# Differential attention and gated layer: a new order of work in the slots, three shared or split PSUM banks, and the gated layer's first steps taken into the last slots

## The chip, the cores and the metric

One Trainium2 chip (trn2), one of its cores. The metric is the device time of one execution of the whole program in microseconds (us); lower is better. The five engines of a core are named as in the profile: PE (matmul; PEld is its weight load), DVE (vector), ACT (scalar), POOL (GpSimd) and SP, which here only issues DMAs.

## What is computed

The program runs six layers, one after the other, on x of 4096 rows of 256 numbers (128 sequences of 32 tokens): `x = x + layer(layernorm(x))`. The change touches two of them, the second (differential attention) and the third (a gated feed-forward with 4-bit weights):

```
def _L0_attn_ref(x, wq, wk, wv, wout, ...):          # 128 sequences of 32 tokens
    q = (x @ wq.T).reshape(b, t, NH2, HALF)           # 4 half heads of 64
    k = (x @ wk.T).reshape(b, t, NH2, HALF)
    v = (x @ wv.T).reshape(b, t, H, 2 * HALF)         # 2 heads of 128
    q = _apply_rope(q, cos, sin)
    k = _apply_rope(k, cos, sin)
    probs = jax.nn.softmax(einsum('bhtd,bhsd->bhts', q, k) / SCALING, axis=-1)
    diff = probs[:, :, 0] - lam * probs[:, :, 1]
    attn = jnp.einsum('bhts,bhsd->bhtd', diff, v)
    attn = attn * jax.lax.rsqrt(jnp.mean(attn * attn, axis=-1, keepdims=True) + EPS)
    return (attn * subln_weight) @ wout.T
...
def _L0_ffn_ref(x, weight1, weight2, weight3):        # the gated layer, 256 -> 704 -> 256
    w1, w2, w3 = (nf4_roundtrip(w) for w in (weight1, weight2, weight3))
    h = jax.nn.silu(x @ w1.T) * (x @ w2.T)
    return h @ w3.T
```

## The kernel before, in words

The rows of x are cut into 32 chunks of 128 rows, four sequences each (`CHUNKS`). Everything is float32; the rounded 4-bit weights come as bf16. Each layer is a `Phase` with one function for each engine, and these are called layer after layer, so every engine has one straight queue, written out by hand in program order; semaphores tie the queues together.

**Differential attention** (tiles ending in `_d`) is a software pipeline over slots n = -3 to 34 (`SLOTS`). In slot n the engines work on chunks n-2 to n+3 at once. PE does, in this order: `qk` (queries and keys of chunk n+1, L1613), `qk_t` (turns of the roped queries and keys of chunk n, L1621), `v` (L1626), `at` (turns of the weighed values of chunk n-2, L1634), `x` (turns of the normalized x of chunk n+2, L1640), `s` (scores of chunk n, L1650), `av` (weighing: the transposed probabilities of chunk n-1 times v, L1660) and `y` (output projection of chunk n-2, L1669). ACT copies PSUM to SBUF and does the exponentials and squares; DVE does rope, softmax, the layernorm's statistics (L1719 to L1721), the normalizing (L1726) and the residual sum (L1781); POOL does half of the rope (L1596, L1597) and two powers of -0.5, `inv_std` (L1600) for the layernorm and `inv_rms` (L1603) for the norm after the weighing. ACT's `attn` (L1677) scales the weighed values by `inv_rms`; `attn_t` (L1696) copies their turns for the output projection.

In the weighing each sequence s of 32 tokens and each head c is one 32x128 product. A product works on the 32 array rows of its sequence, and its place in the output (partitions 32s and up) picks the 32 array columns. Both heads of a sequence use the same 32x32 tile of the array: four tiles, each used twice.

**The gated layer** (tiles ending in `_g`) first turns its weights: 18 parts of W1, W2 and W3, each with PE transposes into a bank (L1917, L1920) and an ACT copy out (L2002 to L2006), four banks in turn. Then come the statistics of four chunks (`statistics`), POOL's powers, the normalizing, the turn of x (L1928, eight transposes), ACT's rounding copy (L2012) and DVE's remainder (L2092). Then the projections run for 8 turns of 512 rows: 11 tiles up (L1964, four matmuls each) and 6 parts down (L1985). PE begins all this only when the last `y_d` has been added (`pe.wait_ge(*before.high)`). SP loads the gated layer's x and weights in `preload`, called in slot 30 of the layer before.

## Time and profile before

| | us |
|---|---|
| median of 3 runs | 3342.03 (3341.38 to 3342.73) |
| the profiled execution | 3341.55 |
| its span, first to last instruction | 3339.5 |
| differential attention, first `qk` to last `y` | 906.2 to 1092.3 |
| gated layer's first up projection | 1099.5 |

All views below are of the profiled execution. Times are from the start of its span. "Granted clock" is the share of TensorE's full clock (2.4 GHz; the lower level is 1.2 GHz, shown as 0.50) that the chip gave it in a stretch. A timeline row is one group of like instructions in a row: start, length from the first start to the last end, engine, line, operation, output and inputs, and how many. Matmuls overlap their neighbours, so PE is read by the starts of its groups. A float32 matmul shows up as two records, which is why counts there are twice those of the program order. In square brackets stands how long the engine was idle before, and on whom it waited.

### The profile page before, as it was taken

Reading aid. Unit: us, or ns where it says so; the run is one execution under the profiler, and the core shown is the slowest. Engines: PE = TensorE matmul, PEld = TensorE weight load, DVE = VectorE, ACT = ScalarE, POOL = GpSimd, SP = SyncE. Lnnn points to the kernel's source line nnn. Section 1 sums busy time; section 2 is a strip of 40 time slices with the busy share of each in tenths; the row PEclk is TensorE's granted clock in tenths of the full one; section 3 lists DMA queues with packets and bytes.
Section 4 is the critical chain, followed back from the end, with each engine's and each line's share of the span. In section 5 each row is a group of like instructions: output and inputs, shape, how many; then the busy total and the mean of one; then the engine's idle time right before and its main releaser. Section 6 shows DMA issues by size and latency. Waiting matters only on the chain.

```text
span 3339.5 us, 103483 instructions
## 1 busy us (share of the span) xinstructions
PE 3287.2 (98%) x34647; PEld 2394.9 (72%) x34656; DVE 2329.3 (70%) x7527; ACT 1988.0 (60%) x6064; POOL 1796.8 (54%) x3701
## 2 busy tenths in 40 slices
PE   9999999999899999999999999999999999999999
PEld 7888888888666777777777777777766655555555
DVE  5677777777788667888888888878868844444443
ACT  5777777777556547777777777777765411111111
POOL 5666666666566447777777777777746500000000
PEclk9999999999999999999999999999999999999999
DMA  3111111111212231111111111111136720000000
GB/s 99 55 58 56 54 54 54 58 55 54 72 43 61 85 125 46 46 49 47 45 46 46 48 46 46 47 44 47 48 90 159 186 66 19 19 17 17 17 16 9
DMA packets 280202, 187.70 MB, mean 56 GB/s; under 512 B 117037, under 2 KB 276997, under 8 KB 280085
## 3 DMA queue, kind: packets, MB, share of 16 engines
q1 hardware_dynamic: 279797, 185.75, 19.9%
q8 instruction: 73, 1.20, 0.2%
q10 hardware_dynamic: 288, 0.40, 0.1%
q14 instruction: 44, 0.36, 0.0%
HBM read 145.61 MB, written 36.21 MB: 54 GB/s over the span
## 4 chain that ended last, share of the span: by engine, by line
PE 57%; DMA 3%; DVE 1%; ACT 0%; SPq 0%; issue 0%; POOL 0%; DVEq 0%; ACTq 0%; POOLq 0%
PE bank_e L2827 13%; PE c_ps_a L1100 7%; PE bank_e L2807 7%; PE b_ps_a L1066 6%; PE s_ps_a L1073 5%; PE out_ps_a L1126 3%; PE a_ps_a L1077 3%; PE c_ps_a L1077 2%; PE b_ps_a L1077 2%; PE out_ps_a L1110 2%; PE c_ps_a L1159 2%; DMA by_dim_q_r<-scratch_q 1%; PE c_ps_a L1138 1%; PE out_ps_a L1197 1%; PE c_ps_a L1149 1%; DMA scratch_q<-proj_t_q_r 1%
## 5 line engine op out<-in xcount | busy, mean ns | idle before, releaser
L1226 ACT ACTIVATE probs_a<-s_ps_a,neg_max_a 128x257 f32<-128x257 f32 x1024 | 473.7, 475 | 83.3 <-DVE neg_max_a L1346 78.5
L1280 POOL TENSOR_SCALAR probs_a<-probs_a,gated_a 128x256 f32<-128x256 f32 x1024 | 470.9, 479 | 26.4 <-POOL gated_a L1289 26.4
L1346 DVE TENSOR_REDUCE neg_max_a<-s_ps_a 128x1 f32<-128x257 f32 x1024 | 424.4, 414 | 0.0
L2870 ACT ACTIVATE gate_e<-bank_e 128x512 f32<-128x512 f32 x128 | 76.3, 597 | 486.1 <-PE bank_e L2827 459.1
L546 POOL TENSOR_SCALAR probs_i<-probs_i,inv_sum_i 128x256 f32<-128x256 f32 x512 | 242.9, 487 | 135.1 <-DVE inv_sum_i L710 130.6
L2768 POOL TENSOR_TENSOR inv_std_e<-var_eps_e,half_e 128x4 f32<-128x4 f32 x8 | 8.1, 1012 | 561.7 <-DVE var_eps_e L2884 561.7
L2994 DVE TENSOR_TENSOR hidden_e<-gate_e,bank_e 128x512 f32<-128x512 f32 x128 | 87.2, 687 | 277.5 <-PE bank_e L2827 274.8
L1345 DVE TENSOR_TENSOR self_s_a<-s_ps_a,mask_a 128x32 f32<-128x32 f32 x1024 | 186.1, 182 | 135.5 <-PE s_ps_a L1073 135.4
L530 ACT ACTIVATE probs_i<-s_ps_i,neg_max_i 128x257 f32<-128x257 f32 x512 | 235.8, 474 | 58.9 <-DVE neg_max_i L781 57.1
L373 PE MATMUL a_ps_i<-w_k_i,ctx_t_i 128*128 128x256 f32 x1024 | 252.4, 389 | 0.0
L1100 PE MATMUL c_ps_a<-w_v_a,ctx_t_a 128*32 128x256 f32 x4096 | 247.6, 382 | 0.0
L360 PE MATMUL c_ps_i<-w_v_i,ctx_t_i 128*128 128x256 f32 x1024 | 247.5, 379 | 0.0
L2827 PE MATMUL bank_e<-xn_t_e,w_gate_e 128*128 128x512 f32 x512 | 241.4, 594 | 0.0
L2827 PE MATMUL bank_e<-xn_t_e,w_up_e 128*128 128x512 f32 x512 | 240.6, 592 | 0.0
L1066 PE MATMUL b_ps_a<-ctx_t_a,w_qk_a 128*128 128x256 f32 x1016 | 240.5, 380 | 0.0
L2807 PE MATMUL bank_e<-w_down_e,hidden_e 128*128 128x256 f32 x1024 | 231.3, 379 | 0.0
L2807 PEld LDWEIGHTS bank_e<-w_down_e,hidden_e 128*128 128x128 f32 x1024 | 194.0, 190 | 50.0 <-issue 26.5
L781 DVE TENSOR_REDUCE neg_max_i<-s_ps_i 128x1 f32<-128x257 f32 x512 | 181.5, 416 | 50.9 <-PE s_ps_i L439 50.1
L1226 ACT ACTIVATION_READ_ACCUMULATOR probs_a<-s_ps_a,neg_max_a 128x1 f32 x1024 | 209.4, 205 | 0.0
L373 PEld LDWEIGHTS a_ps_i<-w_k_i,ctx_t_i 128*128 128x128 f32 x1024 | 184.4, 190 | 28.9 <-issue 0.4
L1100 PEld LDWEIGHTS c_ps_a<-w_v_a,ctx_t_a 128*32 128x32 f32 x4096 | 120.0, 109 | 115.2 <-issue 25.7
L1073 PE MATMUL s_ps_a<-k_t_a,q_bd_a 32*128 32x289 f32 x2048 | 197.6, 455 | 5.1 <-ACT probs_a L1226 3.1
(398 smaller groups left out, 8164.6 us busy)
## 6 DMA issues: line engine op xcount, KB each, us to landing
ctx_t_i<-in_ctx_t SPq DMA_DIRECT2D x128, 256.0 KB, 2.7
ctx_t_a<-in_ctx_t SPq DMA_DIRECT2D x128, 256.0 KB, 2.7
mask_a<-in_L_xattn_mask SPq DMA_DIRECT2D x512, 4.0 KB, 1.5
v_bd_a<-v_self_a SPq DMA_DIRECT2D x512, 8.0 KB, 1.8
x_tok_i<-in_x SPq DMA_DIRECT2D x32, 128.0 KB, 2.0
x_res_i<-in_x SPq DMA_DIRECT2D x32, 128.0 KB, 2.4
x_after<-y_tok_i SPq DMA_DIRECT2D x32, 128.0 KB, 1.8
x_tok_d<-x_after SPq DMA_DIRECT2D x32, 128.0 KB, 2.2
```

Source lines behind the costliest of these rows:

```text
L360: last = pe.matmul(c_ps[:, r * D:r * D + D], ctx_t[at.b(1)][:, c, r * P:r * P + P], w_v[:, c, :], start=c == 0, stop=c == 1)
L373: last = pe.matmul(a_ps[:, r * D:r * D + D], ctx_t[at.b(2)][:, c, r * P:r * P + P], w_k[:, c, :], start=c == 0, stop=c == 1)
L530: act.activation(probs[:, i, :], s_ps[i][:, 0:K], ACT.Exp, bias=neg_max[:, i:i + 1], accum_out=row_sum[:, i:i + 1]).then_inc(exp_done, 1)
L546: pool.tensor_scalar(probs[:, i, 0:2 * P], probs[:, i, 0:2 * P], inv_sum[:, i:i + 1], 1.0, ALU.mult, ALU.mult).then_inc(probs_ready, 1)
L1066: last = pe.matmul(into[:, f * n:f * n + n], w_qk[:, c, D + f * P:D + f * P + P], ctx[:, c, 0:n], start=c == 0, stop=c == 1)
L1073: pe.matmul(s_ps[:, g, 0:N], q_bd[j][rows, f, :, :].rearrange("p h q -> p (h q)"), k_t[j][rows, f, :], start=True, stop=True).then_inc(sco ...
L1100: last = pe.matmul(c_ps[32 * g:32 * g + 32, r * D:r * D + D], ctx_t[at.b()][:, c, r * P + 32 * g:r * P + 32 * g + 32], w_v[:, c, :], start ...
L1226: act.activation(probs[:, t, :], s_ps[:, g, 0:K], ACT.Exp, bias=neg_max[:, t:t + 1], accum_out=row_sum[:, t:t + 1]).then_inc(exp_done, 1)
L1280: pool.tensor_scalar(probs[:, t, 0:2 * P], probs[:, t, 0:2 * P], gated[:, t:t + 1], 1.0, ALU.mult, ALU.mult).then_inc(probs_ready, 1)
L1346: dve.tensor_reduce(neg_max[:, 4 * f + g:4 * f + g + 1], s_ps[:, g, 0:K], AX.X, ALU.max, negate=True).then_inc(max_ready, 1)
L2807: last = pe.matmul(w[:, t * D:t * D + D], hidden[e % 2][:, k, tok:tok + P], w_down[:, e, k, :], start=k == 0, stop=k == TILES - 1)
L2827: last = pe.matmul(w[:, :], weights[:, e, c, t * P:t * P + P], xn_t[:, c, :], start=c == 0, stop=c == 1)
```

## The change

It has four parts.

1. **Banks.** `av_ps` takes two banks, one for each head. `v_ps` and `y_ps` become the two halves of one bank, `vy_ps`. For that, PE's `v` waits until DVE has added the previous `y`, and PE's `y` waits until ACT has copied `v`; and DVE adds `y` right after `ms` and no longer at the end of its slot.
2. **Weighing.** Head 1 of sequence s goes to output partitions 32 x ((s+2) mod 4), so the eight products use eight different tiles. All eight now increase the semaphore (before, four did). The rows of head 1 stand rotated by two sequences in `attn`, which `attn_t` puts right: its one copy of 256 columns becomes two copies of 128. PE does `av` ahead of `s`.
3. **Start of the gated layer.** Its statistics and normalizing of four chunks stand in slots 29 to 32 of DVE and POOL, where the differential layer has none left. Six groups of weight turns (W1 and W2, two parts a group) and their ACT copies stand in slots 30 to 33, and the turn of the first x, ACT's rounding copy and DVE's remainder in slot 33. The W3 turns follow the last `y`; their ACT copies stand between the first SiLUs. The wait for the last `y_d` moves to the third up tile.
4. **SP.** `preload` of the gated layer moves from slot 30 to slot 27, and the second loads of x to slot 33.

```diff
-    qk_ps, v_ps, tx_ps, av_ps = (pb(f"{n}_ps") for n in ("qk", "v", "tx", "av"))
-    s_ps = pb("s_ps", (P, 2, 512))
-    qk_t_ps, y_ps = (pb(f"{n}_ps") for n in ("qk_t", "y"))
+    qk_ps, qk_t_ps, vy_ps, tx_ps = (pb(f"{n}_ps") for n in ("qk", "qk_t", "vy", "tx"))
+    av_ps, s_ps = (pb(n, (P, 2, 512)) for n in ("av_ps", "s_ps"))
+    v_ps, y_ps = vy_ps[:, 0:D], vy_ps[:, D:2 * D]
...
-            if n == CHUNKS - 2:
+            if n == CHUNKS - 5:
                 for j in range(2):
                     sp.wait_ge(stored[j], 16 * 4)
                 ahead.preload(sp)
+            if n == CHUNKS + 1:
+                ahead.second(sp)
...
+            elif n + 3 - CHUNKS in range(LANES):
+                ahead.pool(pool, n + 3 - CHUNKS)
...
+            if n == CHUNKS - 1:
+                ahead.weights[0](pe, 1)
+            if n == CHUNKS:
+                pe.wait_ge(qk_t_ready, CHUNKS)
+                ahead.weights[0](pe, 2)
+                ahead.weights[0](pe, 3)
+            if n == CHUNKS + 1:
+                ahead.weights[0](pe, 4)
+                ahead.weights[0](pe, 5)
+                pe.wait_ge(centred_ready, CHUNKS)
+                ahead.rows[0](pe, 0)
             if live(n + 1):
                 ge(pe, v_ready, n + 1)
+                ge(pe, y_ready, n - 2)
...
+                for s in range(4):
+                    own = slice(L * s, L * s + L)
+                    for c in range(2):
+                        across = (s + 2 * c) % 4
+                        last = pe.matmul(av_ps[L * across:L * across + L, c, 0:P], diff_t[(n - 1) % 2][own, c * L:c * L + L], v[(n - 1) % 3][own, c * P:c * P + P], start=True, stop=True)
+                        last.then_inc(av_full, 1)
...
                 pe.wait_ge(at_ready, n - 1)
                 ge(pe, y_ready, n - 2)
+                if live(n + 1):
+                    pe.wait_ge(v_ready, n + 2)
...
+            if CHUNKS - 1 <= n <= CHUNKS:
+                ahead.weights[1](act, 2 * (n - CHUNKS + 1))
+            if n == CHUNKS + 1:
+                ahead.weights[1](act, 4)
+                ahead.weights[1](act, 5)
...
+            if n == CHUNKS:
+                ahead.weights[1](act, 3)
+            if n == CHUNKS + 1:
+                ahead.rows[1](act, 0)
...
-                act.activation(attn_t[:, :, :].rearrange("p c k -> p (c k)"), at_ps, ACT.Copy).then_inc(at_ready, 1)
+                act.activation(attn_t_of[:, 0::3, :], at_of[:, 0::2, :], ACT.Copy)
+                act.activation(attn_t_of[:, 1:3, :], at_of[:, 1::2, :], ACT.Copy).then_inc(at_ready, 1)
...
+            if n == CHUNKS + 1:
+                ahead.rows[2](dve)
+            if live(n - 2):
+                dve.wait_ge(y_full, n - 1)
+                ge(dve, stored[n % 2], 16 * ((n - 2) // 2))
+                dve.tensor_tensor(y[n % 2][:, :], y_ps, x_tok[(n - 2) % X_TILES][:, :], ALU.add).then_inc(y_ready, 1)
...
+    W_BANKS = [bank[0], bank[0], bank[1], bank[0], bank[1], bank[0], down_ps[0], down_ps[0], down_ps[1]]
+    W_BEFORE = [None, 0, None, 1, 2, 3, None, None, None]
...
-        pe.wait_ge(*before.high)
-        pe.wait_ge(const_ready, 2)
-        for n in range(W_TURNS):
...
+        for group in range(6, 9):
+            turn_weights(pe, group)
...
+                if i == 0 and tile == 2:
+                    pe.wait_ge(*before.high)
...
                 silu(i, n)
+                if i == 0 and n < 3:
+                    copy_weights(act, 6 + n)
```

PE's order in a full slot, before and in the change. PE is the engine that is almost never idle there; `vy_ps_d` with `w_v` is `v`, with `w_o` is `y`.

```order
L1613 MATMUL qk_ps_d<-w_qk_d,xn_t_d 128x512 x2
L1621 MATMUL qk_t_ps_d<-ident_d,qk_d 128x128 x4
L1626 MATMUL v_ps_d<-w_v_d,xn_t_d 128x256 x2
L1634 MATMUL tx_ps_d<-ident_d,attn_d 128x128 x2
L1640 MATMUL tx_ps_d<-ident_d,xn_d 128x128 x2
L1650 MATMUL s_ps_d<-qk_t_d 32x32 x16
L1660 MATMUL av_ps_d<-v_d,diff_t_d 32x128 x8
L1669 MATMUL y_ps_d<-w_o_d,attn_t_d 128x256 x2
```

The same slot in the change:

```order
L1621 MATMUL qk_ps_d<-w_qk_d,xn_t_d 128x512 x2
L1629 MATMUL qk_t_ps_d<-ident_d,qk_d 128x128 x4
L1646 MATMUL vy_ps_d<-w_v_d,xn_t_d 128x256 x2
L1654 MATMUL tx_ps_d<-ident_d,attn_d 128x128 x2
L1662 MATMUL tx_ps_d<-ident_d,xn_d 128x128 x2
L1672 MATMUL av_ps_d<-v_d,diff_t_d 32x128 x8
L1682 MATMUL s_ps_d<-qk_t_d 32x32 x16
L1693 MATMUL vy_ps_d<-w_o_d,attn_t_d 128x256 x2
```

Only `av` and `s` have changed places.

PE at the end of the differential layer, from slot 32's `at` on, before:

```order
L1634 MATMUL tx_ps_d<-ident_d,attn_d 128x128 x2
L1660 MATMUL av_ps_d<-v_d,diff_t_d 32x128 x8
L1669 MATMUL y_ps_d<-w_o_d,attn_t_d 128x256 x2
L1634 MATMUL tx_ps_d<-ident_d,attn_d 128x128 x2
L1669 MATMUL y_ps_d<-w_o_d,attn_t_d 128x256 x2
L1917 MATMUL bank_g<-ident_bf_g,rows_g 128x128 x10
```

And in the change, down to the first up projection:

```order
L1654 MATMUL tx_ps_d<-ident_d,attn_d 128x128 x2
L1672 MATMUL av_ps_d<-v_d,diff_t_d 32x128 x8
L1693 MATMUL vy_ps_d<-w_o_d,attn_t_d 128x256 x2
L1973 MATMUL bank_g<-ident_bf_g,rows_g 128x128 x6
L1973 MATMUL bank_g<-ident_bf_g,rows_g 128x64 x2
L1983 MATMUL bank_g<-ident_g,xn_g 128x128 x4
L1654 MATMUL tx_ps_d<-ident_d,attn_d 128x128 x2
L1983 MATMUL bank_g<-ident_g,xn_g 128x128 x4
L1693 MATMUL vy_ps_d<-w_o_d,attn_t_d 128x256 x2
L1976 MATMUL bank_g<-ident_bf_g,cols_g 128x128 x10
L1976 MATMUL bank_g<-ident_bf_g,cols_g 64x128 x4
L2028 MATMUL bank_g<-xs_g,up_w_g 128x512 x44
```

The last W2 turns and both halves of the x turn have moved ahead of the last `y`; before, all of them, W1's too, followed it.

DVE in a slot of the drain (chunk 31's softmax), in the change:

```order
L1793 TENSOR_REDUCE top_d<-s_ps_d 128x4
L1794 TENSOR_TENSOR centred_d<-s_ps_d,top_d 128x128
L2132 BN_STATS stats_g<-x_tok_g 128x6
L2134 BN_AGGR mean_var_g<-stats_g 128x2
L2136 TENSOR_SCALAR var_eps_g<-mean_var_g 128x1
L1807 TENSOR_SCALAR ms_d<-ss_d 128x2
L1813 TENSOR_TENSOR y_d<-vy_ps_d,x_tok_d 128x256
L1819 TENSOR_REDUCE row_sum_d<-probs_d 128x4
```

Before, `ms_d` followed `centred_d` directly here, `row_sum_d` followed `ms_d`, and `y_d` came last.

## Rows read from the trace of the kernel before

**Rows 1.** Busy time by stretch: us, then each engine's busy time, clock, DMA.

```profile
920.00:1065.00 145.00, 144.47 (x1829) 98.88 (x1828) 118.77 (x397) 89.59 (x321) 100.51 (x107) 0.99 0.15 46
```

**Rows 2.** Timeline of a full slot, PE's groups: start, length, what.

```profile
1000.21 1.88 PE L1613 MATMUL qk_ps_d<-w_qk_d,xn_t_d 128*128 128x512 f32 x4
...
1003.45 0.38 PE L1640 MATMUL tx_ps_d<-ident_d,xn_d 128*128 128x128 f32 x2
...
1003.76 0.35 PE L1650 MATMUL s_ps_d<-qk_t_d 64*32 64x32 f32 x32
...
1004.04 0.65 PE L1660 MATMUL av_ps_d<-v_d,diff_t_d 32*32 32x128 f32 x16
...
1004.62 1.13 PE L1669 MATMUL y_ps_d<-w_o_d,attn_t_d 128*128 128x256 f32 x4
...
1005.59 1.45 PE L1613 MATMUL qk_ps_d<-w_qk_d,xn_t_d 128*128 128x512 f32 x3
```

**Rows 3.** The weighing's matmuls: ns min/median/max of one record.

```profile
L1660 PE MATMUL av_ps_d<-v_d,diff_t_d x512: 267/268/292, 923.3 to 1087.5; 32*32 32x128 f32 x171
```

**Rows 4.** The same slot's timeline: ACT, POOL and DVE.

```profile
1000.35 0.97 POOL L1600 TENSOR_TENSOR inv_std_d<-var_eps_d,half_d 128x1 f32<-128x1 f32 x1 [0.31 <-DVE var_eps_d L1721]
...
1001.30 0.70 POOL L1603 TENSOR_TENSOR inv_rms_d<-ms_d,half_d 128x2 f32<-128x2 f32 x1
...
1002.03 0.62 ACT L1677 ACTIVATE attn_d<-av_ps_d,inv_rms_d 128x128 f32<-128x128 f32 x2 [1.64 <-POOL inv_rms_d L1603]
...
1002.25 0.37 DVE L1726 TENSOR_SCALAR xn_d<-x_tok_d,mean_var_d,inv_std_d 128x256 f32<-128x256 f32 x1
...
1002.53 0.42 DVE L1781 TENSOR_TENSOR y_d<-y_ps_d,x_tok_d 128x256 f32<-128x256 f32 x1
1002.54 0.60 ACT L1682 ACTIVATE qk_raw_d<-qk_ps_d 128x512 f32<-128x512 f32 x1
...
1003.02 0.61 ACT L1685 ACTIVATE qk_t_d<-qk_t_ps_d 128x512 f32<-128x512 f32 x1
...
1003.50 0.40 ACT L1688 ACTIVATE v_d<-v_ps_d 128x256 f32<-128x256 f32 x1
...
1003.92 0.38 ACT L1696 ACTIVATE attn_t_d<-tx_ps_d 128x256 f32<-128x256 f32 x1
...
1004.31 0.29 DVE L1752 TENSOR_REDUCE top_d<-s_ps_d 128x4 f32<-128x128 f32 x1 [0.45 <-PE s_ps_d L1650]
...
1005.52 0.15 DVE L1721 TENSOR_SCALAR var_eps_d<-mean_var_d 128x1 f32<-128x1 f32 x1
```

**Rows 5.** Timeline, slots 30 to 33 and the gated layer's start.

```profile
1078.71 0.38 ACT L1688 ACTIVATE v_d<-v_ps_d 128x256 f32<-128x256 f32 x1 [0.20 <-PE v_ps_d L1626]
...
1078.83 0.36 PE L1650 MATMUL s_ps_d<-qk_t_d 64*32 64x32 f32 x32
1078.99 0.38 ACT L1696 ACTIVATE attn_t_d<-tx_ps_d 128x256 f32<-128x256 f32 x1
...
1083.03 0.36 PE L1650 MATMUL s_ps_d<-qk_t_d 64*32 64x32 f32 x32
...
1089.54 0.62 ACT L1677 ACTIVATE attn_d<-av_ps_d,inv_rms_d 128x128 f32<-128x128 f32 x2 [1.01 <-POOL inv_rms_d L1603]
...
1091.13 1.13 PE L1669 MATMUL y_ps_d<-w_o_d,attn_t_d 128*128 128x256 f32 x4 [0.47 <-ACT attn_t_d L1696]
...
1092.98 3.01 PE L1917 MATMUL bank_g<-ident_bf_g,rows_g 128*128 128x128 bf16 x24 [0.71 <-DVE y_d L1781]
1093.39 1.49 ACT L2004 ACTIVATE up_w_g<-bank_g 128x256 fp32r<-128x256 bf16 x5 [2.31 <-PE bank_g L1917]
...
1097.61 1.78 PE L1928 MATMUL bank_g<-ident_g,xn_g 128*128 128x128 f32 x8
...
1099.50 0.47 PE L1964 MATMUL bank_g<-xs_g,up_w_g 128*128 128x512 f32 x1
```

**Rows 6.** Busy time and granted clock over the gated layer's start (columns as Rows 1).

```profile
1092.00:1099.00 7.00, 6.23 (x47) 4.15 (x46) 4.29 (x19) 5.11 (x19) 2.30 (x4) 0.52 0.33 99
```

More of the change, by code:

```diff
@@ L180 @@
     pool: Callable = None
+    weights: tuple = ()
+    rows: tuple = ()
+    lanes: tuple = ()
 def image_attention(nc, io, stack):
@@ L1635, in tensor @@
                 last.then_inc(at_full, 1)
+            if n == CHUNKS + 1:
+                ahead.rows[0](pe, 1)
             if live(n + 2):
@@ L1756, in vector @@
                 statistics(dve, n + 3)
+            elif n + 3 - CHUNKS in range(LANES):
+                ahead.lanes[0](dve, n + 3 - CHUNKS)
             if live(n + 1):
@@ L1902, in gpsimd, with turn_weights @@
         loads.first_operands(pool)
-    def tensor(pe, before, ahead):
-        pe.wait_ge(*before.high)
-        pe.wait_ge(const_ready, 2)
-        for n in range(W_TURNS):
-            k, f = divmod(n, PARTS + 1)
-            m = P if f < PARTS else REST
-            if f == 0:
-                pe.wait_ge(w_in[k], 32 if k < 2 else 16)
-            if n >= 4:
-                pe.wait_ge(w_ready, n - 3)
-            w = bank[n % 4][:, :].bitcast(BF16)
+    def turn_weights(pe, group):
+        if W_BEFORE[group] is not None:
+            pe.wait_ge(w_ready, W_BEFORE[group] + 1)
+        if group == 0:
+            pe.wait_ge(const_ready, 2)
+        if group % 3 == 0:
+            pe.wait_ge(w_in[group // 3], 32 if group < 6 else 16)
+        w = of_group(group)
+        for j in range(2):
+            k, f = divmod(2 * group + j, PARTS + 1)
+            m = P if f < PARTS else REST
@@ L1923, in turn_x, with turn_half_x, tensor @@
+        last.then_inc(w_turned, 1)
+    def turn_half_x(pe, c, i=0):
+        ge(pe, y_ready, 2 * i - 2)
+        for a in range(LANES):
+            pe.wait_ge(xn_ready, i * LANES + a + 1)
+            last = pe.transpose(x_ps[c][:, a * P:a * P + P], xn[a][:, c * P:c * P + P], ident[:, :])
+        last.then_inc(x_full, 1)
+    def tensor(pe, before, ahead):
+        for group in range(6, 9):
+            turn_weights(pe, group)
         def turn_x(i):
             for c in range(2):
-                ge(pe, y_ready, 2 * i - 2)
@@ L1926, in turn_x @@
-                for a in range(LANES):
-                    pe.wait_ge(xn_ready, i * LANES + a + 1)
-                    last = pe.transpose(x_ps[c][:, a * P:a * P + P], xn[a][:, c * P:c * P + P], ident[:, :])
-                last.then_inc(x_full, 1)
+                turn_half_x(pe, c, i)
         def wait_bank(i, tile):
@@ L2148, in vector @@
         loads.copy_last(dve, down_ps[0], down_ps[1])
-    return Phase(preload, sync, gpsimd, tensor, scalar, vector, (y_ready, 2 * TURNS), (y_ready, 2 * TURNS))
+    return Phase(preload, sync, gpsimd, tensor, scalar, vector, (y_ready, 2 * TURNS), (y_ready, 2 * TURNS), second=second, pool=deviation,
+                 weights=(turn_weights, copy_weights), rows=(turn_half_x, high_of_half_x, low_of_x), lanes=(first_statistics, normalize_row))
 class Turn:
@@ L2469, in tensor, with scalar @@
         turns(pe, turn, looped=False)
-    def scalar(act):
+    def scalar(act, ahead):
         def turn(t):
```

170 lines of the change are left out of this document (94 added, 76 removed).

## The prediction

> **What bounds the kernel now.** I looked first at the busy times of the differential layer. From 920 to 1065 us PE is busy for 144.5 of 145.0 us at a granted clock of 0.99 [rows 1]. DVE, ACT and POOL have gaps (118.8, 89.6 and 100.5 us busy). So the full slots go at PE's pace: from one `qk` to the next 1005.59 - 1000.21 = 5.38 us. The 145 us hold 27 of them; I count 26. The second view is the timeline of such a slot, because an engine that is always busy hides how late the others are. PE's groups follow each other without a gap [rows 2]. ACT waits 1.64 us for POOL's `inv_rms` before `attn`, and DVE 0.45 us for the scores before `top` [rows 4]: the others run a ring of their own inside PE's slot, and it must be known how much of the 5.38 us that ring takes. The third view is the end of the layer [rows 5]. From chunk 30's scores at 1078.83 the last `y` is 12.30 us away (1091.13), and the first up projection of the gated layer another 8.37 us (1099.50). There PE waits, then turns weights at a clock of 0.52 [rows 6], which is mostly the lower level.
>
> **Weighing on eight tiles.** One record takes 0.267 us [rows 3] and the group of 16 takes 0.65 us [rows 2], so the last record starts 0.38 us after the first. Four tiles take 16 records in four rounds, so a round is some 0.38 / 3 = 0.13 us. Eight tiles need two rounds: the last record starts about 0.19 us after the first. The next group now follows 1004.62 - 1004.04 = 0.58 us after the first; it would follow after 0.39 us. PE saves 0.19 us a slot and could do a slot in 5.19 us. Bounds: nothing (if tiles on the same array rows don't run together) to 0.19. I take 0.19: the scores, 32 records on tiles of which four share the same array rows, start and end within 0.35 us although one takes about 0.2 [rows 2].
>
> Twice as many of these matmuls increase a semaphore. The Trainium skill, "TensorE: Matmul & The Clock Gate" (the cost: per-tile semaphore tail), holds that such increments serialize at some 26 ns each. By that, an estimate from its figure, four more would cost 0.1 us, and if it held up the next group the slot below would be 5.50 instead of 5.45 us. No row here sets the increments' cost apart.
>
> **The ring.** Does the slot follow PE down? The scores are the pivot. I add up starts [rows 2, 4], each from the row before it in the chain (those of POOL and ACT belong to the slot before, one slot length off):
> - scores to `top` 0.55, `top` to `var_eps` 1.21, `var_eps` to `inv_std` 0.23 (1005.52 less 5.38 is 1000.14, `inv_std` at 1000.35; rounded);
> - `inv_std` to `inv_rms` 0.95, to `attn` 0.73, to `qk_raw` 0.51, to `qk_t` 0.48: 4.66 so far;
> - `qk_t` takes 0.61, and a semaphore 0.05: scores again after 5.32 us.
>
> So the slot can't fall below 5.32 whatever PE saves. A second ring takes two slots. It leaves the first at `qk_t` (4.66) and goes on: `v` 0.48; `attn_t` 0.33; `attn_t` done 0.48; semaphore 0.05; `y` to the next `qk` 1005.59 - 1004.62 = 0.97; `qk` to the scores 3.55, plus 0.39, since the weighing now stands ahead of them. That is 10.91 us, 5.45 a slot. The same sum before: `attn_t` 0.42 after `v` and 0.38 long, without the 0.39: 10.51, or 5.26, under PE's 5.38. Two terms are not in the rows. `v` to `attn_t` lies between 0.28 (slot 30 [rows 5], with no x to wait for) and 0.42; I take 0.33, near the first, since the turn of x will be over by then. The split `attn_t` lies between 0.38 (the whole copy) and 0.62 (`attn`, also two of 128 columns); I take 0.48, since `attn` also scales. A third ring goes through DVE: `y`'s 0.35 us now lie ahead of `xn`. `top` to the start of `xn` is 3.32, plus 0.35, plus 0.37 for `xn`, plus 0.05, then the turn of x to the weighing 0.31, the weighing 0.39, and 0.55 to `top`: 5.34 us. It is not the longest, but close.
>
> So the full slot goes from 5.38 to **5.45 us** (5.38 with both terms low, 5.57 with both high): 26 x 0.07 = **+1.8 us** (0 to +5). The sharing of a bank costs nothing by these numbers: `y` is added some 0.6 us before PE's next `v`, and `v` is copied about 0.4 us before `attn_t` is; cover gone, either would lengthen a slot by what it is late.
>
> **The last slots.** Taken away from behind the last `y`: W1's and W2's turns (3.0 us) and the two-part turn of x with its copies (1097.61 to 1099.50, 1.9 us) [rows 5], and the wait for `y_d` (0.7). Left are W3's 14 turns. From the last `y` to the first projection it was 8.37 us; now `y` 1.1 and the turns 0.8 at full clock: 1.9 to 2.7 us.
>
> Against it stand the slots themselves. They have no PE bound; each engine's queue is the path.
> - Slot 30: the weighing lies ahead of the scores of chunk 30: +0.4.
> - Slot 31: the new statistics on DVE (some 0.55 us, as in `top` to `var_eps` [rows 4]) lie ahead of `qk_d`, and POOL's `inv_std_g` (0.95) ahead of `inv_rms`, so that `attn` and behind it `qk_t` and the scores of chunk 31 come about 0.9 later than 4.20 us after the last scores (1083.03 - 1078.83).
> - Slot 32: statistics, `y` and `inv_std_g` again lie ahead of chunk 30's `attn` and chunk 31's softmax: +0.5.
> - Slot 33: two groups of weight copies (four of 0.3 us, 1.49 / 5 [rows 5]) lie ahead of the last `attn`, half covered by its wait of 1.01 for POOL: +0.7; ACT's first rounding copy stands between `attn` and `attn_t`, mostly beside PE's turns.
>
> Together +2.1 for the distance of 12.30 us, and +0.4 for slot 30. At full clock: 8.37 - 2.1 = 6.3 saved, 2.5 spent, -3.8 us. The clock: before, the lower level lay over the turns [rows 6]. The drain will again have PE idle, and a stretch at the lower level will then lie over W3's turns, the turn of x and perhaps the first projections; I charge 1.2 us (0 to 3). Tail: **-2.6 us** (-4.5 to 0).
>
> `preload` three slots earlier costs nothing: its DMAs take SP about 5 us, the store queued behind them (`y` of chunk 25) has two slots, 10.8 us, before its buffer is used again, and nothing else is queued on SP. W3's six ACT copies (1.8 us) lie between SiLUs of a layer whose PE has 11 us of projections first; uncovered they would cost that much once.
>
> **Sum.** +1.8 - 2.6 = -0.8 on the profiled execution's 3341.55, so 3340.8. The median before is 0.5 above that execution: 3341.3 us.
>
> **The rivals.**
> *PE's saving is kept.* If the ring has more give than its starts suggest (semaphore hops overlapped, x no longer held), the slot sits near PE's 5.19: 26 x -0.19 = -4.9, tail -3.5: 3333.6 us. For it: PE is the one engine without gaps [rows 1]. Against: two rings sum to 5.32 and 5.34 already. Chance 0.13.
> *The ring through `attn_t` is at its high end, slower than before.* Split copy 0.62, `v` to `attn_t` 0.42, several waits ahead of `y` (0.14), and eight tiles no faster than four: 10.91 + 0.14 + 0.09 + 0.09 + 0.19 = 11.42, or 5.71: +8.6, less a tail of -1.5: 3349.1 us. It decides against the change from a slot of 5.48 us on, where 26 x 0.10 eats the tail. Chance 0.09.
> *The drain gives it all back.* The lower clock lies over the first projections, and slots 31 to 33 grow by 4 instead of 2 us: tail about +0.5, 3344.3 us. For it: PE already waits there, 0.47 us for the last `attn_t` [rows 5], and every new step stands in front of one of the drain's own. Chance 0.16.
> *The change doesn't do what it says:* the steps stand in PE's order as described, so this is left only for the tiles, in the rival above.
> Forecast: 0.62, of itself from 3337 to 3345.
>
> **How the numbers follow.** A difference of 0.2% (6.7 us) is taken as the least that can be told from no change. The forecast, and nearly all of the third rival, lie within it. Faster: 0.13 of the first rival and 0.02 of the forecast's lower edge, 0.15. Slower: most of the second rival, 0.08. Same: 0.77. The range takes in the first rival, whose place is known, and the third: 3333.5 to 3346.5, which leaves about 0.1 out.
>
> **What would show it.** A slot near 5.45 with PE waiting in front of `y` for ACT's `attn_t` shows the second ring; waiting in front of the turn of x for `xn`, the third; PE without waits and 5.2, the first rival. The distance from `av` to the scores near 0.39 shows the eight tiles. From the scores of chunk 30 to the first projection I expect 16.5 to 18 us in place of 20.67. Wrong would be: the steps in the drain finding gaps where I stack them, or a clock that stays up.

## The result and the profile after

The changed kernel takes 3346.97 us (median of 20 runs, 3342.55 to 3351.47), the kernel before in the same rounds 3341.29 us. The ratio is 1.0017, with a 95% interval of 1.0010 to 1.0023. The forecast was 3341.3 us, so it is 5.7 us short, and the time lies 0.5 us outside its range. By the forecast's own measure of 0.2% this is still no change; but the interval lies clear of 1, so the kernel did get a little slower. The profiled execution has a span of 3345.5 us, 6.0 us more than before. One execution of a kernel below (`e_slots_alone`, 4889 us at a mean granted clock of 0.64) is left out everywhere.

Four milestones from the traces say where the 6 us arise, in us from the span's start:

| | before | after | difference |
|---|---|---|---|
| last `qk` projection of the differential layer | 1075.50 | 1078.36 | +2.9 |
| first up projection of the gated layer | 1099.50 | 1098.68 | -0.8 |
| last matmul of the adapter layer | 2478.87 | 2477.43 | -1.4 |
| last matmul of the reshaped attention layer | 2661.36 | 2667.40 | +6.0 |

At the end of the stretch that the change touches, the difference is the forecast's -0.8 us. (The first layer, in which nothing is changed, ends within 0.1 us of itself in these two traces; over the 16 traces below its end scatters by 2.6 us, so one milestone alone says little.) It is -1.4 us up to the end of the adapter layer. Then the reshaped layer, in which no line is changed, takes 190.0 us from the last adapter matmul to its own last one, where it took 182.5.

Busy time by stretch in the changed kernel (us, then each engine's busy time, granted clock, DMA share and GB/s), for [rows 1] and [rows 6]:

```profile
920.00:1065.00 145.00, 144.39 (x1774) 95.18 (x1772) 116.25 (x389) 86.36 (x338) 98.20 (x104) 1.00 0.16 46
...
1092.00:1099.00 7.00, 5.98 (x59) 4.25 (x59) 3.40 (x10) 5.79 (x19) 1.25 (x2) 1.00 0.42 128
```

PE is as busy as it was. But the clock over the gated layer's start is 1.00, where it was 0.52.

A full slot on the timeline of the changed kernel, for [rows 2] and [rows 4]:

```profile
1003.93 0.37 DVE L1767 TENSOR_SCALAR xn_d<-x_tok_d,mean_var_d,inv_std_d 128x256 f32<-128x256 f32 x1
...
1004.36 0.44 PE L1662 MATMUL tx_ps_d<-ident_d,xn_d 128*128 128x128 f32 x2
1004.38 0.61 ACT L1721 ACTIVATE qk_t_d<-qk_t_ps_d 128x512 f32<-128x512 f32 x1
...
1004.73 0.45 PE L1672 MATMUL av_ps_d<-v_d,diff_t_d 32*32 32x128 f32 x16
1004.86 0.41 ACT L1724 ACTIVATE v_d<-vy_ps_d 128x256 f32<-128x256 f32 x1
1005.11 0.58 PE L1682 MATMUL s_ps_d<-qk_t_d 64*32 64x32 f32 x32
1005.12 0.31 ACT L1732 ACTIVATE attn_t_d<-tx_ps_d 128x128 f32<-128x128 f32 x1
1005.28 0.32 ACT L1733 ACTIVATE attn_t_d<-tx_ps_d 128x128 f32<-128x128 f32 x1
...
1005.65 1.13 PE L1693 MATMUL vy_ps_d<-w_o_d,attn_t_d 128*128 128x256 f32 x4
1005.78 0.29 DVE L1793 TENSOR_REDUCE top_d<-s_ps_d 128x4 f32<-128x128 f32 x1 [0.56 <-PE s_ps_d L1682]
```

From the weighing to the scores it is 1005.11 - 1004.73 = 0.38 us. The scores' group, however, takes 0.58 us, where it took 0.35 [rows 2], and `top` comes 0.67 us after its start instead of 0.55 (0.68 over the full slots). `y` starts when the scores are through; `attn_t` has been done since 1005.60. The slot is 5.51 us.

Whom does PE wait for in it? The list of waits of the same stretch, 920 to 1065 us (us in total, times, longest), has this:

```profile
ACT attn_d L1709 <- POOL inv_rms_d L1611: 42.6, 26, 1.8
...
PEld qk_t_ps_d L1629 <- DVE qk_d L1804: 7.3, 26, 1.1
```

The weight load that waits there for `qk_d` delays nothing: PE is still busy with the `qk` matmuls. The wait that sets the slot is too short for this list, which leaves out those under 0.15 us, and is read from ends and starts. `xn` ends at 1003.93 + 0.37 = 1004.30, and the turn of x starts at 1004.36. In all but the first two slots of this stretch (25 of 27) the turn's weight load starts 0.05 us after the end of `xn`. `qk_t` ends at 1004.38 + 0.61 = 1004.99, and the scores start only at 1005.11, 0.38 us after the weighing, as the eight tiles give. So PE's scores wait for the weighing, the weighing for the turn of x, and this for DVE's `xn`: the prediction's third ring.

The layer's end, on PE alone, for [rows 5]:

```profile
1082.69 0.36 PE L1682 MATMUL s_ps_d<-qk_t_d 64*32 64x32 f32 x32 [0.16 <-ACT qk_t_d L1721]
...
1087.79 0.58 PE L1682 MATMUL s_ps_d<-qk_t_d 64*32 64x32 f32 x32
...
1096.83 1.13 PE L1693 MATMUL vy_ps_d<-w_o_d,attn_t_d 128*128 128x256 f32 x4
1097.80 0.95 PE L1976 MATMUL bank_g<-ident_bf_g,cols_g 128*128 128x128 bf16 x14
1098.68 2.60 PE L2028 MATMUL bank_g<-xs_g,up_w_g 128*128 128x512 f32 x10
```

The first up projection comes 15.99 us after the scores of chunk 30. It was 20.67, and 16.5 to 18 were expected.

What is new in the reshaped layer is seen on PE's timeline. The kernel before:

```profile
2560.27 1.98 PE L2361 MATMUL m_ps_r<-xn_t_r,w_k_r 128*128 128x512 f32 x4
2562.18 1.69 PE L2376 MATMUL s_ps_r<-k_rows_r,by_dim_q_r 64*32 64x128 f32 x64
2563.80 1.98 PE L2361 MATMUL m_ps_r<-xn_t_r,w_k_r 128*128 128x512 f32 x4
```

The changed kernel, the same three groups:

```profile
2559.75 1.98 PE L2445 MATMUL m_ps_r<-xn_t_r,w_k_r 128*128 128x512 f32 x4
2561.66 0.89 PE L2460 MATMUL s_ps_r<-k_rows_r,by_dim_q_r 64*32 64x128 f32 x36
2564.74 0.68 PE L2460 MATMUL s_ps_r<-k_rows_r,by_dim_q_r 64*32 64x128 f32 x28 [2.18 <-issue]
2565.35 3.64 PE L2445 MATMUL m_ps_r<-xn_t_r,w_k_r 128*128 128x512 f32 x4
```

A group of 32 score matmuls (64 records, two to a matmul) has no wait inside. It stops after 36 records for 2.18 us, with no releaser ("issue"). The projection behind it then takes 3.64 instead of 1.98 us. Its stretch in the table of windows:

```profile
2565.30:2568.70 3.40, 3.40 (x12) 1.51 (x5) 3.07 (x5) 0.00 (x0) 3.37 (x4) 0.50 0.02 5
```

So after PE has stood, the granted clock is 0.50, the lower level. The kernel before has one such stretch of 3.4 us in this layer, the changed one three. (Their number doesn't follow the layer's length closely: the changed kernel's second trace below has two at 189.1 us, and kernel j has two of 6.8 us each at 183.0.) The waits of PE's weight loads for the scores from 2476 to 2668 us are, before and after:

```profile
PEld s_ps_r L2376 <- issue: 13.3, 17, 2.3
```

```profile
PEld s_ps_r L2460 <- issue: 18.7, 18, 2.7
```

Those are 5.4 us more of standing without a releaser. The DMA view of the changed kernel for 0.3 us around the point where PE stops, 2562.40 to 2562.70 (queue, kind: packets, MB, share), has this:

```profile
q8 instruction: 1, 0.02, 20.0%
```

It is one read of 16384 bytes of instructions. It starts at 2562.48, lasts 0.96 us and is followed by PE's restart at 2564.74. The view doesn't name the engine; that these reads of queue 8 are PE's I infer from the stops that go with them in every kernel below.

### The profile page after: what moved, and what is told of

Its sections match the earlier page's. It is cut to its first block, busy times and chain, and to the rows that moved or that the text cites. A ratio compares the mean times of both kernels' runs of the same rounds, so it can differ in the third digit from the quotient of the medians.

```text
span 3345.5 us, 103553 instructions
## 1 busy us (share of the span) xinstructions
PE 3289.9 (98%) x34656; PEld 2392.3 (72%) x34656; DVE 2331.6 (70%) x7527; ACT 1988.3 (59%) x6096; POOL 1801.3 (54%) x3701
## 4 chain that ended last, share of the span: by engine, by line
PE 59%; DMA 1%; DVE 1%; issue 0%; ACT 0%; POOL 0%; SPq 0%; DVEq 0%; POOLq 0%; ACTq 0%
PE bank_e L2911 13%; PE c_ps_a L1103 7%; PE bank_e L2891 7%; PE b_ps_a L1069 6%; PE s_ps_a L1076 5%; PE out_ps_a L1129 3%; PE a_ps_a L1080 3%; PE c_ps_a L1080 2%; PE b_ps_a L1080 2%; PE out_ps_a L1113 2%; PE c_ps_a L1162 2%; PE m_ps_r L2445 1%; PE c_ps_a L1141 1%; PE out_ps_a L1200 1%; PE c_ps_a L1152 1%; PE s_ps_r L2460 1%
```

## The experiments

Two questions were open: what lengthens an untouched layer, and why the slot is 5.51 and not 5.45 us. The table has all runs: the instructions of PE in the built program, the slot, the reshaped layer (last adapter matmul to last reshaped one, from the one profiled execution of each), after how many of 64 score records PE stops in the same group of scores (the second group of the layer's fourth turn of 512 rows), and the median with the interval of the ratio to before in the same rounds.

| kernel | PE instr. | slot | reshaped | stops after | time | ratio, 95% |
|---|---|---|---|---|---|---|
| before | 6044 | 5.38 | 182.5 | 51 | 3341.29 | |
| after | 6073 | 5.51 | 190.0 | 36 | 3346.97 | 1.0010-1.0023 |
| after_again | 6073 | 5.51 | 189.1 | 36 | 3346.26 | 1.0003-1.0021 |
| a_scores_first | 6073 | 5.32 | 188.6 | 36 | 3339.99 | 0.9990-1.0008 |
| d_gated_start_alone | 6045 | 5.38 | 183.6 | 50 | 3336.44 | 0.9974-0.9992 |
| e_slots_alone | 6072 | 5.51 | 187.7 (again) | 37 | 3352.04 | 1.0021-1.0042 |
| f_before_29_more | 6044 | 5.38 | 182.6 | 51 | 3339.50 | 0.9991-1.0011 |
| g_after_29_fewer | 6073 | 5.51 | 190.8 | 36 | 3347.04 | 1.0009-1.0029 |
| h_scores_first_29_fewer | 6073 | 5.33 | 186.7 | 36 | 3339.09 | 0.9992-1.0011 |
| c_four_tiles | 6073 | 5.69 | 190.0 | 36 | 3351.65 | 1.0022-1.0047 |
| b_x_between | 6073 | 5.71 | 186.6 | 36 | 3352.01 | 1.0021-1.0046 |
| i_before_29_real | 6072 | 5.38 | 189.4 | 37 | 3346.95 | 1.0007-1.0027 |
| j_after_29_less | 6045 | 5.51 | 183.0 | 50 | 3342.18 | 0.9990-1.0009 |
| k_scores_first_29_less | 6045 | 5.32 | 183.6 | 50 | 3335.98 | 0.9974-0.9993 |
| m_before_14_more | 6058 | 5.38 | 191.7 | 44 | 3348.44 | 1.0011-1.0031 |
| l_before_56_more | 6099 | 5.38 | 183.8 | 23 | 3345.41 | 1.0002-1.0021 |

**The changed kernel a second time**, for the scatter.

> The changed kernel once more, unaltered, to see which of its stages repeat. Theory A (the profiled execution's +7.5 us in the reshaped attention layer is a property of the changed program): the stage from the last adapter matmul to the routing is again 190 us or more, and the total 4 to 7 us above before's. Rival C (that stage scatters from one execution to the next, and the median of 20 runs is shifted by chance): the stage comes out nearer to before's 184 to 187 us in this profile, and the difference of the medians of these rounds is within -2 to +3 us. Up to the last adapter matmul both expect -1.4 us against before, within 0.3.

It gave 3346.26 us and the same milestones: the first up projection at 1098.41 (after 1098.68), the reshaped layer 189.1 us. So the lengthening belongs to this program and is no scatter. The table bears this out: the five traces with 6044 or 6045 instructions have 182.5 to 183.6 us there, the nine with 6072 or 6073 have 186.6 to 190.8.

**Scores ahead of the weighing**, the rest as changed:

```diff
             if live(n + 2):            # turn of x
...
-            if live(n - 1):            # weighing, eight tiles
-...
             if live(n):                # scores
...
+            if live(n - 1):            # weighing, eight tiles
+...
```

> The changed kernel with PE's scores ahead of the weighing again, as before the change; eight tiles, banks and everything else of the change stay. Theory A (the scores are slow because they follow 32 short matmul records directly, and they stand on the ring through qk_t): the scores' group is back at 0.35 us from 0.58, the slot falls from 5.51 to 5.25 to 5.38 us, and the scores follow the turn of x by 0.31 us. The weighing's own group then becomes longer than 0.45 us, since it is the one that follows 64 short records. Rival (the slot is set by ACT's split copy or by y ahead of xn, not by the scores' place): the slot stays above 5.45 us.

```profile
1007.97 0.36 PE L1672 MATMUL s_ps_d<-qk_t_d 64*32 64x32 f32 x32
1008.26 0.49 PE L1683 MATMUL av_ps_d<-v_d,diff_t_d 32*32 32x128 f32 x16
1008.68 1.13 PE L1693 MATMUL vy_ps_d<-w_o_d,attn_t_d 128*128 128x256 f32 x4
```

The scores take 0.36 us again, and the slot is 5.32 us, exactly the sum of the forecast's first ring. PE waits for `qk_t` (7.0 us in 26 slots), and the scores start 0.05 us after its end: now it is the first ring that sets the slot. The order of weighing and scores costs the changed kernel 0.19 us a slot.

**The gated layer's start alone**, with the full slots as before:

```diff
-    qk_ps, qk_t_ps, vy_ps, tx_ps = (pb(f"{n}_ps") for n in ("qk", "qk_t", "vy", "tx"))
-    av_ps, s_ps = (pb(n, (P, 2, 512)) for n in ("av_ps", "s_ps"))
+    qk_ps, v_ps, y_ps, tx_ps, av_ps, qk_t_ps = (pb(f"{n}_ps") for n in ("qk", "v", "y", "tx", "av", "qk_t"))
+    s_ps = pb("s_ps", (P, 2, 512))
```

(and with them the scores first, four tiles, one copy to `attn_t`, `y` added last on DVE)

> Parts 3 and 4 of the change alone: the gated layer's statistics, weight turns and first x in slots 29 to 33, with the differential layer's slots as before (scores before weighing, four tiles, v and y in banks of their own, y added last, one copy for attn_t); only the banks are numbered anew. Theory A (each part acts where it stands): full slots at 5.38 us as before, first up projection some 4.5 us earlier than in the kernel before, and all later stages earlier by as much. Rival B (the early start costs later stages time): the projection is earlier all the same, but the reshaped attention layer, from the last adapter matmul on, takes more than before's 182 us by 5 us or more, and the total is at or above before's.

The first up projection comes at 1094.96, 4.5 us earlier than before, as expected, and the kernel takes 3336.44 us, less than both. Beside slots as they were, the steps moved into the last slots are worth more than the 2.6 us that the forecast gave them.

**The changed slots alone**, with the gated layer's start as before (all `ahead.weights`, `ahead.rows`, `ahead.lanes` and `ahead.pool` steps taken out of the slots again).

> Parts 1 and 2 of the change alone: banks, eight tiles, weighing before the scores, y added earlier, split copy; the gated layer starts as before, after the last y. Theory A: full slots at 5.51 us as in the changed kernel, so 26 x 0.13 = 3.4 us more up to the last qk, and the total 3 to 5 us above before's. Rival B (the total's increase belongs to the early start of the gated layer): the total at most 3.5 us above before's, the reshaped layer as long as before.

> A second look at the changed slots with the gated layer's start as before (3352.8 us in its first runs; TensorE's stream has 6072 instructions). Both parts of the account: slots 5.51 us (+3.4 us by the last qk projection), the drain as slow as before, so first up projection 5 to 6 us later than before, and the reshaped layer 188 to 191 us instead of 182.5; 3350 to 3354 us in all.

It takes 3352.0 us, 11 us more than before, so both expectations of the first run missed. The second run's 3353.1 us came out as said, its two parts just outside what was said. In its trace the slots are 5.51 us, the first up projection comes 6.6 us later than before, and the reshaped layer takes 187.7 us: 6.6 + 5.2 = 11.8 us in all. Of the 6.6, 4.1 are there at the last `qk` projection, behind the slots. The other 2.5 arise in the drain, where the granted clock is 0.50 for 17.1 us (6.8 in the kernel before); what kept it down so long was not tried. The rest is the reshaped layer's.

**Is it the place of PE's instructions?** The changed kernel has 29 more instructions on PE than the kernel before (28 of them by its slots, as e shows, and one by the new drain, as d shows), and the layer is written out for PE (it is a loop for the others). I first tried to shift the stream by 29 waits.

```diff
 f: before, ahead of the output projection
+                if live(n + 1):
+                    pe.wait_ge(v_ready, n + 2)
 g (after) and h (a_scores_first), at the weighing
-                pe.wait_ge(v_ready, n)
+                if not (live(n - 3) and live(n)):
+                    pe.wait_ge(v_ready, n)
```

> The kernel before with one more wait ahead of each slot's output projection (for a value that has long been copied by then), 29 in all: TensorE's instruction stream then has as many instructions ahead of the adapter and the reshaped layers as the changed kernel's has; nothing else is changed. Theory A (the reads of TensorE's instructions come at other places of the unrolled reshaped layer because 29 instructions stand before it): slot 5.38 us as before or up to 0.06 longer, the last adapter matmul to the last reshaped one 188 to 190 us instead of 182.5, holes of 2 us or more inside the groups of scores s_ps_r, and the time 3346 to 3349 us. Theory B (the reshaped layer is longer because of when it starts or how the slots ended, not because of where its instructions stand): 182 to 184 us there, and 3340 to 3343 us in all.

> The changed kernel without 29 waits that an earlier wait of the same engine already covers (the weighing's wait for v, which the output projection of the slot before has waited past), so that TensorE's stream has as many instructions ahead of the later layers as the kernel before. Theory A (place in the instruction stream): slot still 5.51 us, or up to 0.05 shorter, the last adapter matmul to the last reshaped one 182 to 184.5 us instead of 190, no hole of 2 us inside a group of scores beyond the one at the first weighing that the kernel before has too, and 3339.5 to 3342 us in all. Theory B (start or phase): 189 to 190 us there and 3346 to 3348 us in all.

> The changed kernel with the scores' group ahead of the weighing, and without the same 29 waits. With the waits it took 3340.0 us, slot 5.32, reshaped layer 188.6 us. Theory A: reshaped layer 182 to 184.5 us, 3333 to 3336 us in all, ahead of both kernels. Theory B: 188 to 189 us and 3339 to 3341 us.

All three stayed at the times of their models, which looks like the fall of theory A. It is not: the built programs have 6044, 6073 and 6073 instructions on PE, as their models have. A second and a third wait of a matmul share one instruction, so nothing was shifted. What the three do give is a second execution of each: 182.6, 190.8 and 186.7 us.

**The same, with the instructions counted.**

```diff
 i: before, ahead of the projection of v (m: only where n % 2)
                 ge(pe, v_ready, n + 1)
+                ge(pe, ss_ready, n - 2)
 l: i, and ahead of the first projection
+                ge(pe, ss_ready, n - 2)
+                ge(pe, rms_ready, n - 3)
 j (after) and k (a_scores_first), ahead of the output projection
-                ge(pe, y_ready, n - 2)
-                if live(n + 1):
-                    pe.wait_ge(v_ready, n + 2)
+                if not live(n + 1):
+                    ge(pe, y_ready, n - 2)
```

> The kernel before with one more wait ahead of each slot's projection of v, for squares that were taken a slot earlier, so that it never holds; unlike in the last attempt the build turns it into an instruction of its own in TensorE's stream in 28 slots: counted in the built program, that stream has 6072 instructions where the kernel before has 6044 and the changed kernel 6073 (the attempt with the wait ahead of the output projection had 6044, since a second and a third wait share one instruction). Theory A (where TensorE's instructions stand decides how long the unrolled reshaped layer takes): slots 5.38 to 5.42 us, last adapter matmul to last reshaped one 188 to 191 us, 3346 to 3349 us in all. Theory B (start time, phase, or the memory that the layers before left): 182 to 184 us, and 3340 to 3342 us in all.

> The changed kernel with two waits less ahead of each slot's output projection (for y's add, which the projection of v in the same slot has waited for, and for the copy of v, which stands ahead of the copy to attn_t on ScalarE): TensorE's stream has 6045 instructions instead of 6073. Theory A: slots 5.51 us, at best 0.05 shorter; the reshaped layer 182 to 184.5 us instead of 189 to 191; 3339.5 to 3342 us in all. Theory B: 189 to 191 us and 3346 to 3348 us in all.

> The same two waits less in the kernel with the scores ahead of the weighing (slot 5.32 us; reshaped layer 188.6 and 186.7 us in two executions, 3339 to 3340 us in all, 6073 instructions on TensorE). Theory A: 182 to 184.5 us there, 3332 to 3336 us in all. Theory B: 186 to 189 us and 3338 to 3340 us.

The kernel before with 28 idle instructions more takes 3346.95 us, as long as the changed kernel, and its slots stay at 5.38. The changed kernel with 28 fewer takes 3342.18. The reshaped layer goes from 182.5 to 189.4 us in the one and from 190.0 to 183.0 in the other. Where PE stops, first in i, then in j:

```profile
2564.70 0.89 PE L2377 MATMUL s_ps_r<-k_rows_r,by_dim_q_r 64*32 64x128 f32 x37
2567.78 0.68 PE L2377 MATMUL s_ps_r<-k_rows_r,by_dim_q_r 64*32 64x128 f32 x27 [2.19 <-issue]
2568.39 3.47 PE L2362 MATMUL m_ps_r<-xn_t_r,w_k_r 128*128 128x512 f32 x4
```

```profile
2558.59 1.08 PE L2459 MATMUL s_ps_r<-k_rows_r,by_dim_q_r 64*32 64x128 f32 x50
2560.08 0.48 PE L2459 MATMUL s_ps_r<-k_rows_r,by_dim_q_r 64*32 64x128 f32 x14 [0.41 <-issue]
2560.49 1.98 PE L2444 MATMUL m_ps_r<-xn_t_r,w_k_r 128*128 128x512 f32 x4
```

28 instructions are 14 pairs of records (a load and a product each), and the stop has moved from the 51st to the 37th. Kernel k, with the scores first and 28 instructions less, is the fastest with 3335.98 us, level with d.

> The kernel before with the wait of the run with 28 more instructions in every second slot only: 6058 instructions on TensorE (before 6044, that run 6072). If each instruction more shifts the reads and the lengthening grows with the shift: 184 to 188 us from the last adapter matmul to the last reshaped one, 3342 to 3346 us in all. If it is a matter of one position falling inside a group of scores, it is either as before (182 to 184, 3340 to 3342) or as with 28 (188 to 191, 3346 to 3349).

> The kernel before with that wait and, ahead of each slot's first projection, two more that never hold: 6099 instructions on TensorE, 55 more than before. If the reshaped layer's length depends on where the reads of 256 instructions fall, it is another value than 182.5 or 189.4 or one of the two, 181 to 192 us, and slots stay at 5.38 to 5.45 us. If what lengthened it was the number of waits as such, it is 194 to 197 us. 3340 to 3350 us in all.

Kernel m, then l:

```profile
2563.46 0.95 PE L2378 MATMUL s_ps_r<-k_rows_r,by_dim_q_r 64*32 64x128 f32 x44
2566.58 0.89 PE L2378 MATMUL s_ps_r<-k_rows_r,by_dim_q_r 64*32 64x128 f32 x20 [2.17 <-issue]
```

```profile
2564.62 0.66 PE L2379 MATMUL s_ps_r<-k_rows_r,by_dim_q_r 64*32 64x128 f32 x23
2566.27 0.93 PE L2379 MATMUL s_ps_r<-k_rows_r,by_dim_q_r 64*32 64x128 f32 x41 [0.99 <-issue]
```

With 14 more the stop is after the 44th record (7 earlier), with 55 more after the 23rd. The length of the layer does not grow with the shift: 191.7, 189.4 and 183.8 us for 14, 28 and 55. The number of waits is therefore not the cause; the place is. Kernel l still takes 4.1 us more than before, and only 1.3 of them arise in this layer: its first up projection is 2.4 us late, its first layer already ends 1.6 us late, and its drain has the lower clock for 13.7 us.

**Why the scores are slow.** One run puts the turn of x between weighing and scores, one takes the eight tiles back (`across = s`, one copy to `attn_t`) and leaves the order.

```diff
 b
-            if live(n + 2):            # turn of x, ahead of the weighing
-...
             if live(n - 1):            # weighing
...
+            if live(n + 2):            # turn of x
+...
             if live(n):                # scores
 c
-                        across = (s + 2 * c) % 4
+                        across = s
```

> The changed kernel with the turn of x moved from ahead of the weighing to between weighing and scores, so that 96 short loads and products no longer come in one row (32, then 2 long ones, then 64). If the scores' group of 0.58 us is slow because the short instructions before it used up what had been fetched: scores' group back at 0.35 to 0.45 us, but it starts 0.25 us later after the weighing; the weighing starts 0.3 us earlier or waits for diff_t, so slot 5.40 to 5.50 us. If it is slow for another reason (the eight tiles, the start of the scores ahead of their data): group still 0.55 us or more, slot 5.55 to 5.65 us. TensorE's stream has 6073 instructions, so by theory A the reshaped layer takes 187 to 191 us; 3344 to 3350 us in all.

> The changed kernel with the weighing's two products of a batch on the same tile of four, as before, and the copy to attn_t in one piece again; the weighing still stands ahead of the scores. Theory 1 (two products behind each other on a tile cost the group 0.2 us, as the forecast took it, and the scores behind are slow because 96 short loads and products come in a row): start of weighing to start of scores 0.58 instead of 0.38 us, the scores' group 0.35 to 0.45 us since their instructions have caught up meanwhile, slot 5.50 to 5.60 us. Rival (eight tiles are what makes the scores slow): scores' group back at 0.35 us, start of scores to top 0.56, slot 5.35 to 5.40 us, 3342 to 3344 us in all. In the first case 3346 to 3349 us.

First b, then c:

```profile
1008.06 0.45 PE L1666 MATMUL av_ps_d<-v_d,diff_t_d 32*32 32x128 f32 x16
1008.44 0.44 PE L1672 MATMUL tx_ps_d<-ident_d,xn_d 128*128 128x128 f32 x2
1008.80 0.36 PE L1682 MATMUL s_ps_d<-qk_t_d 64*32 64x32 f32 x32
1009.47 1.13 PE L1693 MATMUL vy_ps_d<-w_o_d,attn_t_d 128*128 128x256 f32 x4 [0.31 <-ACT attn_t_d L1733]
```

```profile
1007.12 0.66 PE L1672 MATMUL av_ps_d<-v_d,diff_t_d 32*32 32x128 f32 x16
1007.71 0.55 PE L1682 MATMUL s_ps_d<-qk_t_d 64*32 64x32 f32 x32
```

In b two longer matmuls stand between the short groups, and the scores are back at 0.36 us. In c the weighing is slower (the scores follow after 0.59 us) and the scores are slow all the same, against the 0.35 to 0.45 us that I expected. So it is the row of 48 short loads and 48 short products without a longer one between them, and not the eight tiles. Neither kernel pays, and both slots are longer than I had expected: b's is 5.71 us, and there PE waits for `attn_t` in front of `y`, the forecast's second ring; c's is 5.69, again with the turn of x 0.05 us behind `xn`.

## Why the prediction was wrong

**What failed: the sum ended at the gated layer's first projection.** Its terms give -0.8 us, and -0.8 us is what the traces have there, by luck: two errors of 1.1 us cancelled (below). The forecast then carried this to the end of the program, since no line behind it changes. But 29 more instructions on PE (28 of them a second wait ahead of a projection of `v`, which the shared bank needs) move every later instruction in PE's stream. The forecast has no term for it, and so puts it at nothing without a reason. The reshaped layer takes 7 us more for it: shown by i (+6.9) and j (-7.0) in opposite directions, by m and l for the place against the number. No rival had this. The second rival's 3349.1 us is near the measured time, but its mechanism is not what happened: its slot was 5.71.

**Eight tiles: right.** The scores follow the weighing after 0.38 us, for 0.39. In c, with four tiles, it is 0.59, and the slot 0.18 longer. The Trainium skill's rule, which the prediction weighed ("TensorE: Matmul & The Clock Gate", the cost: per-tile semaphore tail), had led to an estimate of 5.50 us for the slot, and the slot is 5.51. Yet the traces don't bear the rule out as the reason: the group behind the eight increments starts after the 0.38 us of eight tiles. And with four tiles the next group starts after 0.59 us with eight increments (c) and after 0.58 with four [rows 2].

**The slot: mis-sized by 0.06 us, and the wrong ring.** The second ring's terms hold: `v` to `attn_t` 0.26 us for 0.33, the split copy done after 0.48 for 0.48. It was the third ring that grew, from 5.34 to 5.51. Its step from the scores to `top` is 0.68 instead of 0.55, since the scores' group is 0.58 long. Its step from the turn of x to the weighing is 0.37 instead of 0.31; why was not tried. Its other steps hold: 3.66 from `top` to `xn` for 3.67, 0.37, 0.05 and 0.38 for 0.39. 5.34 + 0.13 + 0.06 = 5.53, or 5.51 with all steps as measured. The prediction took the first step from the row of before [rows 2], where the scores come ahead of the weighing, and didn't ask whether the new place would change their length. The first ring has some 0.07 us to spare at the scores. With the scores first (a) the weighing is no longer part of the third ring, and the first sets the slot, at the forecast's 5.32. Up to the last `qk` the longer slots cost 2.9 us, for 1.8.

**The tail: mis-sized by 1.1 us the other way.** From the last `qk` to the first up projection it was 24.0 and is 20.3 us: -3.7, for -2.6. The path at full clock was charged nearly rightly, -3.8 us: the last `y` comes 14.14 us after the scores of chunk 30, for 14.4, and the first projection 1.85 after it, for 1.9 (the forecast's sum then used 2.1). Slot 30 grew by 1.0 and not by 0.4. What didn't come is the lower clock, charged at 1.2: the stretch at 0.52 [rows 6] is at 1.00. PE now has turns between the last slots' groups; whether that kept the clock up was not tried apart. The traces side with it but not without exception: of the ten with the new drain six have no lower clock there and four (b, c, h, k) have it for 3.4 us; the six with the old drain have it for 6.8 to 17.1 us. The two errors, +1.1 in the slots and -1.1 in the tail, cancelled.

**Preload and W3's copies: free**, as said. From the first up projection to the last adapter matmul the changed kernel takes 0.6 us less than the kernel before, which is within the scatter of these traces.

**How long PE stands.** The traces show when each read of 16384 bytes starts and ends. For the stop of the table (times in us; the stop is counted from the start of the last record ahead of it to the start of the next):

| kernel | read starts | ends | PE goes on | after the read's end | stop |
|---|---|---|---|---|---|
| before | 2560.72 | 2562.13 | 2563.40 | 1.27 | 0.40 |
| j | 2557.77 | 2558.73 | 2560.08 | 1.36 | 0.68 |
| l | 2563.93 | 2564.93 | 2566.27 | 1.35 | 1.26 |
| after | 2562.48 | 2563.44 | 2564.74 | 1.29 | 2.45 |
| m | 2564.20 | 2565.16 | 2566.58 | 1.42 | 2.44 |
| i | 2565.40 | 2566.38 | 2567.78 | 1.40 | 2.45 |

The same holds for all 46 stops over 0.2 us that this group and the ones two and four turns later have in the 16 traces: PE goes on 1.2 to 1.6 us after the read's end, though the stops last from 0.2 to 2.8 us. So the length of a stop is a matter of when its read starts: from 2.4 us before PE gets there to 0.3 us after. The start isn't given by the place alone. After the 35th record, two turns later, the changed kernel's two traces have stops of 1.3 and 1.7 us, and kernel g, with as many instructions, 2.5.

**What stays open.** That PE stands until a read of its instructions has come is shown by these rows, and so is the place. Not shown is why the read starts late at one place and early at another. The data rate of 2558 to 2565 us in 40 steps, before and after:

```profile
GB/s 164 223 281 211 234 234 246 269 258 240 222 211 293 345 375 457 345 345 310 258 281 287 275 328 334 316 339 339 211 135 59 23 23 23 23 82 345 415 339 310
```

```profile
GB/s 222 211 234 234 281 281 228 193 222 304 369 369 386 386 380 386 386 375 386 386 392 380 363 240 141 141 0 0 0 0 0 0 47 334 357 345 339 76 0 0
```

In the changed kernel the read starts at 2562.48, at the 26th step, when the data have just run out. In the kernel before, the read for the same stop starts at 2560.72, in the midst of the data, over 2 us ahead of need. Whether it is asked for later, or waits behind data, was not tried. The read of `after`'s third such stop, at 2651.54, starts as late with data still moving, so waiting for the end of the data can't be the whole answer.

The Trainium skill, "Advanced Engine Details and Errata", ISA Cache, says that an engine's instructions are cached in lines of 16 KB, or 256 instructions. The trace agrees as far as it goes: each read has 16384 bytes, and the stop moves by as many instructions as were added. By that rule 14 instructions can matter and 256 wouldn't; no run here tried 256.

## What to carry to other kernels

Count the instructions of each engine's stream in the built programs of before and after, and where a long written-out stretch of short matmuls follows, treat a shift of a dozen instructions as a risk of several microseconds either way (14 more cost 7 us here). Before blaming or crediting a change for a small difference, compare milestones layer by layer; where an untouched layer moves, shift the stream by idle instructions (and count that they are really there) to tell place from cause. A group of short matmuls must be costed behind the neighbour that it will have, not the one that it had. Where several rings lie within a few tenths of a us of each other, look for the start that follows the end it waits for by the same few hundredths in every slot; a list of waits can leave such short ones out.

## What the runs showed of the hardware

- PE can stop within a group that has no wait: for 2.18 us after the 36th of 64 score records in the changed kernel, with a 16384-byte read of instructions beginning at that moment. It goes on 1.2 to 1.6 us after such a read has ended (46 stops in 16 traces). The granted clock is then 0.50 for 3.4 us, which makes the four records of a 128x512 projection take 3.64 instead of 1.98 us. The same work of the layer takes from 182.5 to 191.7 us in the 16 traces.
- Short matmuls behind short matmuls start more slowly from some point on. Behind the weighing's 16 records the scores' product records start 7 ns apart for some 20 records (each of 0.2 us), then two by two every 43 ns. In b, behind two longer matmuls, they start at most 8 ns apart to the end.
- In the built programs a matmul with one wait carries it itself; a second and a third together cost one instruction more (28 with two waits instead of one gave 28, 29 with three instead of two gave none).
